# Two transformer layers on one core: input split straight from PSUM, key copies on ScalarE, shift products and low parts moved, last sum on TensorE

## The chip, the cores and the metric

The kernel runs on one core of a Trainium2 chip, in one launch. The time is what the device takes from start to end, in microseconds, as the median of several runs. The engines of the core are TensorE (PE in the profile, its weight loads PEld), VectorE (DVE), ScalarE (ACT), GpSimd (POOL) and SyncE (SP, which here only issues transfers). Each runs its own list of instructions in order, and they wait for one another through semaphores.

## What is computed

1024 tokens (32 sequences of 32) of width 128 pass through two layers. Cut to what matters:

```
x = x + moe16(moe8(x, cond))             # layer 0: 8 experts (2 of them taken) + a shared one, then 16 (4 taken) + a shared one
a = ln(attention(ln(x) * g_norm))        # layer 1: 16 heads of 64 queries, one key/value head, one extra null key
                                         # q, k = l2norm(..)*scale; sim = 8 q k + rel_pos_bias + null bias, causal
w, idx = top_k(a @ router_W + b, 2);  gates = softmax(w)
h = ((a - mean) * rstd)[:, :, None] * ln_g + ln_b            # one norm per expert (8 experts)
y = gelu(h @ W1 + b1) @ W2 + b2 + a
out = x + sum_e gates_e * y_e
```

## The kernel before

Every large product is made exact to fp32 with three matrix products of the reduced type fp32r: a number x is split into a high part (a cast) and a low part (x minus the cast), and `three` (L903 to L905) adds high*high, low*high and high*low. So each operand costs a cast, mostly on ScalarE, and a subtraction, on VectorE or GpSimd. Tokens are held as two halves of 512 or eight tiles of 128. There is no scheduler: each engine's list is written out by hand, and the order of the statements in a block is the order in which the engine takes them.

The stages, in the order of time:

1. Layer 0's experts (to about 72 us): a loop over blocks of up-projections (`up_unit`, six products of 128x512 each, two PSUM buffers), ScalarE evaluating the gate half (L703) and VectorE multiplying (`f_unit`, L1457). VectorE also does the routing of the 16 experts between these units, one small linked step after another. After four of the units stands a `shift_bias(e)` (L1024): four small fp32 products W1ᵀ·ln_b of layer 1's expert e, written to PSUM bank 6. `first_bias(0)` (L1513) on VectorE adds b1 to them.
2. The down-projection of layer 0 (L1069), and the norm of layer 1. `turn_tiles` (L1055) turns normed tokens to PSUM; `turned` on VectorE multiplies them by g_norm into `act_T` (L1316), `copy_hi` on ScalarE casts (L641), `query_low` on VectorE subtracts (L1584).
3. The query loop (90 to 124 us) over tiles t. TensorE: `q_rows(t+2)`, `q_turn(t)` (L1123). ScalarE: `q_root` (L736), `q_squares` (L731), `q_turned` (L740). VectorE: `q_sum` (L1595), `q_norm` (L1603). Keys and values come from `kv_rows(s)` (L1102), are copied out of PSUM by VectorE (`key_rows`, L1578) and ScalarE (`value_rows`, L757), and the keys, normed on GpSimd, go back through `turn_keys` and `turned_keys` (L749, L752) into `k_diag`, which all scores need.
4. The attention loop (124 to 173 us): `scores`, `values` (L1209), `project` (L1221); VectorE sums, transposes and norms (L1673 to L1679); GpSimd does `subtract`, `probs` (L590) and `both_rstd` (L608 to L611). Into this loop GpSimd's list also has `split_w2(0)` at t=1, `split_w2(1)` at t=2 (L596) and `low_w1(7)` at t=3 (L537, L539): low parts of weights of layer 1's experts.
5. Layer 1's experts (to 266 us): 16 steps `m_up(k)`, `m_down(k)` of twelve products each, ScalarE's gelu, VectorE's `split_gelu` (L1753, L1757), `weighed` (L1772, product times gate, into `y_tmp`) and `gathered` (L1783, into `y_acc`). The gates are made on VectorE (`route_half(s)`, which ends with a count on `v_z`, then `gates_half(s)`), turned on TensorE (`turn_half_gates`), and spread over all partitions by way of DRAM.
6. The end: transposes of `y_acc` (L1296), the sum with x (L1806), and two output transfers (L447).

What SyncE issues is one list too, and its order matters here. Where it is cut to the second half of the program it reads:

```python
for e in range(M_EXP):                    # W2 of layer 1, L416 to L421
    sp.wait_ge(pool_w1, e + 1)
    sp.wait_ge(act_w1, e + 1)
    sp.wait_ge(pe_b1, e + 1)
    sp.dma_start(w2_stage[:, e], ...)
store_gates(0)                            # L426: waits for v_combT 1, writes 16 KB, waits for it
sp.wait_ge(pe_wo, TILES)
for e in range(6):
    spread_gates(e, 0)                    # L431: 256 KB each, read by weighed
store_gates(1)
```

`pool_w1` counts the `low_w1(e)` that GpSimd has finished. TensorE's list in step 2 of layer 1's experts is `m_up(3)`, `turn_half_gates(1)` (waits for `gates_half(1)`), `m_down(2)` (waits for `weighed(0)` and for `split_gelu(2)`), and VectorE's is `route_half(1)`, `weighed(0)`, `gates_half(1)`, `split_gelu(2, 0)`.

## Time and profile before

| | |
|---|---|
| three runs | 272.82, 275.73 (median), 276.0 us |
| the profiled execution | 273.56 us, of which the span in the trace is 271.8 us |
| busy: PE, DVE, ACT, POOL | 250.7 (92%), 215.9 (79%), 146.3 (54%), 105.3 us (39%) |
| chain that ended last | PE 72%, DVE 13%, POOL 8%, ACT 3% |
| DMA | 14.51 MB, mean 53 GB/s |

TensorE is busy nine tenths of the time, so most of what other engines do lies beside it. Its idle time is in few places: the query loop, the attention loop and the last 6 us. The granted clock is full except in two short stretches. Times in the rows below are microseconds from the span's start; a duration can overlap the next row's start, since instructions are pipelined.

### The profile page before, as it was taken

To read this page: it belongs to the slowest core of one execution; us is meant where nothing else is said; L and a number is where in the kernel's file an instruction comes from. 1 tells how busy PE (TensorE), PEld (TensorE's weight loads), DVE (VectorE), ACT (ScalarE), POOL (GpSimd) and SP (SyncE) were. 2 spreads that over 40 slices of the span, in tenths; PEclk is the share of its full clock that TensorE was granted. 3 is DMA by queue.
4 is the path that set the end of the run, shared out by engine and by line. 5 is a ranking of instruction groups with operands and counts; after the bars stand their busy time and mean duration, and the time that the engine had idled before them with its cause. 6 is when DMAs were issued, how large, how long until landed. Compare 5 with 4: busy or idle time off the path is not lost.

```text
span 271.8 us, 5203 instructions
## 1 busy us (share of the span) xinstructions
PE 250.7 (92%) x1876; PEld 201.0 (74%) x1876; DVE 215.9 (79%) x436; ACT 146.3 (54%) x244; POOL 105.3 (39%) x146
## 2 busy tenths in 40 slices
PE   7898999999999969678999979999999999999992
PEld 6776467867899848567767656878888888888881
DVE  7797868687877498977688677789998888788884
ACT  1675332246630435696444336298687867877550
POOL 2898410133592657632457783622031101101000
PEclk9999999999999997999999979999999999999997
DMA  6993610010300050000300010005192000000002
GB/s 170 240 264 46 220 50 0 5 39 0 52 0 2 0 159 0 0 2 2 113 9 2 2 42 0 2 0 177 64 288 97 2 0 1 0 0 2 1 0 78
DMA packets 25018, 14.51 MB, mean 53 GB/s; under 512 B 11809, under 2 KB 21702, under 8 KB 24993
## 3 DMA queue, kind: packets, MB, share of 16 engines
q1 hardware_dynamic: 24448, 13.89, 18.8%
q0 software_dynamic: 544, 0.29, 0.8%
q8 instruction: 15, 0.25, 0.4%
q14 instruction: 11, 0.08, 0.1%
HBM read 13.55 MB, written 0.62 MB: 52 GB/s over the span
## 4 chain that ended last, share of the span: by engine, by line
PE 72%; DVE 13%; POOL 8%; ACT 3%; issue 2%; POOLq 0%; DVEq 0%
PE ps L903 16%; PE ps L905 16%; PE ps L904 15%; PE ps L1069 5%; PE ps L1000 3%; PE ps L1024 3%; DVE arena L1603 2%; PE ps L964 2%; PE ps L1221 2%; PE ps L1209 2%; PE ps L1151 2%; POOL w_lo L506 2%; POOL rstd L611 2%; POOL arena L590 1%; PE ps L912 1%
## 5 line engine op out<-in xcount | busy, mean ns | idle before, releaser
L843 ACT ACTIVATE att_bias<-ps,bias 128x512 f32<-128x512 f32 x64 | 43.5, 689 | 12.6 <-PE ps L905 12.5
L903 PE MATMUL ps<-act_hi,w_hi 128*128 128x512 f32 x120 | 48.6, 405 | 0.9 <-DVE arena L1364 0.7
L905 PE MATMUL ps<-act_hi,w_lo 128*128 128x512 f32 x120 | 47.0, 392 | 0.0
L904 PE MATMUL ps<-act_lo,w_hi 128*128 128x512 f32 x120 | 46.9, 391 | 0.0
L1757 DVE TENSOR_TENSOR g_lo<-att_bias,g_hi 128x1024 fp32r<-128x1024 f32 x32 | 40.9, 1289 | 0.6
L903 PEld LDWEIGHTS ps<-act_hi,w_hi 128*128 128x128 f32 x120 | 22.5, 188 | 6.4 <-issue 1.8
L905 PEld LDWEIGHTS ps<-act_hi,w_lo 128*128 128x128 f32 x120 | 22.5, 188 | 5.1
L904 PEld LDWEIGHTS ps<-act_lo,w_hi 128*128 128x128 f32 x120 | 22.6, 188 | 4.3
L703 ACT ACTIVATE xc<-ps 128x512 f32<-128x512 f32 x18 | 10.7, 597 | 17.2 <-PE ps L905 17.2
L1414 DVE TENSOR_TENSOR arena<-arena,ps 128x512 f32<-128x512 f32 x24 | 16.1, 683 | 3.4 <-PE ps L964 3.3
L1069 PEld LDWEIGHTS ps<-f_down,arena 128*128 128x128 f32 x144 | 17.8, 192 | 0.6
L1753 DVE CAST g_hi<-att_bias 128x1024 fp32r<-128x1024 f32 x16 | 11.3, 708 | 8.6 <-ACT att_bias L843 8.5
L1069 PE MATMUL ps<-f_down,arena 128*128 128x128 f32 x144 | 18.1, 275 | 0.0
L596 POOL TENSOR_TENSOR w_lo<-w_stage,w_hi 128x512 fp32r<-128x512 f32 x4 | 5.2, 1311 | 31.4 <-ACT w_hi L800 31.4
L850 ACT ACTIVATE g_hi<-att_bias 128x1024 fp32r<-128x1024 f32 x16 | 17.0, 1063 | 0.5
L1221 PE MATMUL ps<-w_out,arena 128*128 128x128 f32 x128 | 17.1, 291 | 0.0
L1457 DVE TENSOR_TENSOR arena<-xc,ps 128x512 f32<-128x512 f32 x18 | 12.4, 687 | 5.7 <-PE ps L905 5.3
L1221 PEld LDWEIGHTS ps<-w_out,arena 128*128 128x128 f32 x128 | 16.4, 207 | 0.3
L506 POOL TENSOR_TENSOR w_lo<-w_stage,w_hi 128x256 fp32r<-128x256 f32 (+1 forms) x16 | 12.6, 819 | 10.3 <-ACT w_hi L647 5.7
L537 POOL TENSOR_TENSOR r_big<-w_stage,vec 128x512 f32<-128x512 f32 x8 | 8.3, 1042 | 17.8 <-ACT w_hi L697 10.7
L596 POOL TENSOR_TENSOR w2b_lo<-w_stage,w2b_hi 128x512 fp32r<-128x512 f32 x4 | 5.6, 1410 | 23.5 <-ACT w2b_hi L800 23.5
L1209 PE MATMUL ps<-arena,v_tok 32*64 32x256 f32 x128 | 10.7, 404 | 3.7 <-DVE arena L1667 2.3
(285 smaller groups left out, 587.8 us busy)
## 6 DMA issues: line engine op xcount, KB each, us to landing
arena<-gate_m SPq DMA_DIRECT2D x16, 256.0 KB, 5.9
w_stage<-in_L_ffn_W SPq DMA_DIRECT2D x9, 256.0 KB, 3.1
w_stage<-in_L_ffn_W SPq DMA_DIRECT2D x1, 1792.0 KB, 8.0
x_tok<-in_x SPq DMA_DIRECT2D x2, 256.0 KB, 3.1
w_stage<-in_L_ffn_w_gate SPq DMA_DIRECT2D x1, 512.0 KB, 4.9
w_stage<-in_L_ffn_w_up SPq DMA_DIRECT2D x1, 512.0 KB, 6.7
w_stage<-in_L_cond_Wq SPq DMA_DIRECT2D x1, 512.0 KB, 6.5
f_down<-in_L_ffn_w_down SPq DMA_DIRECT2D x1, 512.0 KB, 5.9
```

Of the source, the lines that this page charges most:

```text
L506: pool.tensor_tensor(c(w_lo), c(w_stage), c(w_hi).bitcast(f32), ALU.subtract).then_inc(pool_lo, 1)
L843: act.activation(gelu[:, k % 2, b, :], bank(b), ACT.Gelu, bias=bias1[:, c:c + 1])\
L850: act.activation(g_hi[:, k % 2, 2:4, :], gelu[:, k % 2, 2:4, :], ACT.Copy).then_inc(act_ghi, 1)
L903: pe.matmul(dst, wh, xh, start=first, stop=False)
L904: pe.matmul(dst, wh, xl, start=False, stop=False)
L905: return pe.matmul(dst, wl, xh, start=False, stop=last)
L1069: return pe.matmul(bank(6 + s)[:, t * P:(t + 1) * P], f_hid[:, b, cols], f_down[:, b, :], start=first, stop=last)
L1209: pe.matmul(ps[h * DH:(h + 1) * DH, 4 + s // 2, (s % 2) * HB * LEN:(s % 2 + 1) * HB * LEN], v_tok[rows, t, :], pT_buf[rows, t % 2].rearran ...
L1221: pe.matmul(bank(6)[:, 0:P], att_T[:, t % 2, b, :], w_out[:, b, :], start=(b == 0), stop=False)
L1414: dve.tensor_tensor(hid[:, q, cols], hid[:, q, cols], bank(4 + i % 2), ALU.mult).then_inc(v_mul, 1)
L1457: dve.tensor_tensor(f_hid[:, b, s * HW:(s + 1) * HW], g_sb[:, n % 2], bank(2 * (n % 2) + 1), ALU.mult)\
L1757: dve.tensor_tensor(g_lo[:, k % 2, b, :], gelu[:, k % 2, b, :], g_hi[:, k % 2, b, :].bitcast(f32), ALU.subtract).then_inc(v_glo, 1)
```

## The change

- The four `shift_bias(0..3)` leave the expert loop of layer 0 and stand in TensorE's list in the query loop; `first_bias(0)` moves there too, on VectorE. They now wait until ScalarE has copied the first half's keys and values out of bank 6, and `turn_keys` waits for `first_bias(0)`.
- The input of queries: ScalarE casts straight from PSUM with the scale (`input_high`), VectorE makes the low part from PSUM in one instruction (`query_low`), and ScalarE writes the full-precision `act_T` afterwards (`input_scaled`), which `kv_rows` waits for.
- Both key copies go from VectorE to ScalarE; `kv_rows(1)` moves from after `q_turn(1)` to ahead of `q_rows(4)`; `turned_keys(0)` is spread over two turns of the loop, and `turned_keys(1)` and `(2)` stand after it.
- On GpSimd `split_w2(0)` and `(1)` move to t=6 of the attention loop, and `low_w1(7)` behind `low_half(1)`, with a wait for the third count of `v_z`.
- The last step's product is weighed in two halves and added by TensorE with the identity (`last_sum`) instead of by VectorE; the output goes out in three transfers.

```diff
@@ gpsimd
-                if t in (1, 2):
-                    split_w2(t - 1)
-                if t == 3:
-                    low_w1(M_EXP - 1)
                 if t == 6:
                     low_half(0)
+                    split_w2(0)
+                    split_w2(1)
             low_half(1)
+            pool.wait_ge(v_z, 1 + HALVES)
+            low_w1(M_EXP - 1)
@@ scalar
+            def input_high(s):
+                act.wait_ge(pe_xT, 2 + s + 1)
+                act.wait_ge(v_small, 4)
+                cols = slice(s * HW, (s + 1) * HW)
+                act.activation(act_hi[:, cols], bank((4, 7)[s]), ACT.Identity, scale=vec[:, V_GN:V_GN + 1])\
+                    .then_inc(act_hi_s, 1)
+            def input_scaled(s):
+                act.wait_ge(v_lo, 4 + s + 1)
+                cols = slice(s * HW, (s + 1) * HW)
+                act.activation(act_T[:, cols], bank((4, 7)[s]), ACT.Identity, scale=vec[:, V_GN:V_GN + 1])\
+                    .then_inc(act_x, 1)
...
+            def key_rows(s):
+                act.wait_ge(pe_kv, s + 1)
+                act.activation(k_tok[:, s * HT:(s + 1) * HT, :],
+                               bank(6 + s).rearrange("p (t c) -> p t c", c=P)[:, :, 0:DH], ACT.Copy).then_inc(act_k, 1)
...
+            key_rows(0)
+            value_rows(0)
             input_std(1)
             for t in range(TILES):
                 if t == 2:
-                    copy_hi(5)
+                    input_high(1)
+                    input_scaled(1)
...
+                if t == 2:
+                    key_rows(1)
                 if t == 3:
-                    value_rows(0)
                     value_rows(1)
...
-                if 5 <= t:
-                    turned_keys(t - 5)
+                if t in (5, 6):
+                    turned_keys(0, (t - 5,))
+            turned_keys(1)
+            turned_keys(2)
@@ tensor, expert loop of layer 0
-                if 3 <= j < 7:
-                    shift_bias(j - 3)
@@ tensor, query loop
             for t in range(TILES):
                 if t == 1:
                     turn_tiles(1)
+                if t == 2:
+                    shift_bias(1)
+                    kv_rows(1)
                 if t + 2 < TILES:
                     q_rows(t + 2)
+                if t == 1:
+                    shift_bias(0)
                 if t == TILES - 1:
                     scores(0)
                 q_turn(t)
-                if t == 1:
-                    kv_rows(1)
+                if t in (2, 3):
+                    shift_bias(t)
@@ tensor, end
+            for t in range(HT):
+                pe.matmul(last_sum(t), y_acc[:, 1, t * P:(t + 1) * P], ident[:, :], start=(t % 2 == 0), stop=False)
+            for t in range(HT):
+                if t % 2 == 0:
+                    pe.wait_ge(v_y, steps + t // 2)
+                mm = pe.matmul(last_sum(t), y_tmp[:, (steps - 1) % 2, t * P:(t + 1) * P], ident[:, :],
+                               start=False, stop=(t % 2 == 1))
...
@@ vector
             rp_norm(1)
-            first_bias(0)
...
+                dve.scalar_tensor_tensor(act_lo[:, cols], bank((4, 7)[s]), vec[:, V_GN:V_GN + 1],
+                                         act_hi[:, cols].bitcast(f32), ALU.mult, ALU.subtract).then_inc(v_lo, 1)
...
                 if t == 1:
-                    dve.wait_ge(pe_xT, 4)
-                    turned(1, bank(7), 4, scale=vec[:, V_GN:V_GN + 1], lo=False)
-                if t == 2:
-                    key_rows(0)
-                    key_rows(1)
+                    query_low(1)
+                if t == 4:
+                    first_bias(0)
```

How GpSimd's list changes between the attention loop and the end; L596 is `split_w2`, L537 and L539 are `low_w1`, L602 is `low_half`, L590 is `probs`:

```order
 L611 TENSOR_TENSOR rstd<-var,half_neg 128x2 [waits pool_chain]
-L537 TENSOR_TENSOR r_big<-w_stage,vec 128x512 [waits pool_w1,act_w1]
-L539 TENSOR_TENSOR w_lo<-r_big,w_hi 128x512 [waits pool_chain]
 L590 TENSOR_TENSOR arena<-arena,ssum 128x512 [waits v_pT,v_rs]
...
 L602 TENSOR_TENSOR act_lo<-act_T,act_hi 128x512 [waits act_xhi]
+L596 TENSOR_TENSOR w_lo<-w_stage,w_hi 128x512 [waits act_w2]
+L596 TENSOR_TENSOR w2b_lo<-w_stage,w2b_hi 128x512 [waits act_w2]
...
 L602 TENSOR_TENSOR act_lo<-act_T,act_hi 128x512 [waits act_xhi]
+L537 TENSOR_TENSOR r_big<-w_stage,vec 128x512 [waits pool_w1,act_w1,v_z]
+L539 TENSOR_TENSOR w_lo<-r_big,w_hi 128x512 [waits pool_chain]
```

`low_w1(7)` stood ahead of a `probs` in the middle of the attention loop and now stands behind everything of that loop, with a wait for `v_z`.

SyncE's list is not touched there; in the changed program it reads (L422 is the transfer of W2, L427 `store_gates`, L432 `spread_gates`):

```order
L422 DMA w_stage<-in_L_ffn_W 128x4x128 [waits pe_b1,act_w1,pool_w1] x8
L427 DMA gate_m<-comb_T 32x128 [waits v_combT]
L432 DMA arena<-gate_m 128x512 [waits pe_wo,ld_gate_mw]
L432 DMA arena<-gate_m 128x512 x5
L427 DMA gate_m<-comb_T 32x128 [waits v_combT]
```

All eight transfers of W2 stand ahead of the first `store_gates`, as before.

TensorE's list in the query loop from `q_turn(1)` to `q_rows(4)`, before:

```order
L1123 MATMUL ps<-ident,arena 128x128 [waits act_qT,v_qhat]
L1123 MATMUL ps<-ident,arena 128x128 x7
L1102 MATMUL ps<-w_kv,act_T 128x128 [waits v_T,ld_kv]
L1102 MATMUL ps<-w_kv,act_T 128x128 x3
L903 MATMUL ps<-w_hi,act_hi 128x512 [waits pool_lo,v_qhat,v_lo,act_hi_s]
```

and now (L1051 is `shift_bias`, L1149 `q_turn`, L1126 `kv_rows`):

```order
L1051 MATMUL ps<-vec,w_stage 128x96 [waits act_k,act_v,v_small,ld_w1]
L1051 MATMUL ps<-vec,w_stage 128x96 x3
L1149 MATMUL ps<-ident,arena 128x128 [waits act_qT,v_qhat]
L1149 MATMUL ps<-ident,arena 128x128 x7
L1051 MATMUL ps<-vec,w_stage 128x96 [waits act_k,act_v,v_small,ld_w1]
L1051 MATMUL ps<-vec,w_stage 128x96 x3
L1126 MATMUL ps<-w_kv,act_T 128x128 [waits act_x,ld_kv]
L1126 MATMUL ps<-w_kv,act_T 128x128 x3
L929 MATMUL ps<-w_hi,act_hi 128x512 [waits pool_lo,v_qhat,v_lo,act_hi_s]
```

Two shift products stand ahead of `kv_rows(1)`. On ScalarE `key_rows(1)` stands ahead of `q_root(3)`, so that this root waits for `kv_rows(1)` as well.

## Rows read from the trace of the kernel before

**Rows 1.** Windows: window, length, busy us of PE, PEld, DVE, ACT, POOL, granted clock, DMA share, GB/s

```profile
101.20:105.40 4.20, 3.80 (x13) 3.14 (x14) 4.17 (x6) 1.71 (x3) 4.20 (x4) 0.59 0.02 5
158.20:164.00 5.80, 5.43 (x39) 4.32 (x39) 4.85 (x14) 2.77 (x6) 3.78 (x7) 0.71 0.12 35
200.00:266.00 66.00, 66.00 (x290) 53.81 (x288) 55.96 (x70) 46.30 (x62) 6.97 (x5) 1.00 0.08 29
```

**Rows 2.** Timeline of PE in layer 0's expert loop: start, duration, line, [idle before]

```profile
50.32 1.03 PE L1024 MATMUL ps<-vec,w_stage 128*128 128x96 f32 x8
51.13 0.47 PE L903 MATMUL ps<-act_hi,w_hi 128*128 128x512 f32 x1
```

**Rows 3.** Timeline of DVE in the same loop

```profile
48.30 0.69 DVE L1457 TENSOR_TENSOR arena<-xc,ps 128x512 f32<-128x512 f32 x1 [0.77 <-PE ps L905]
52.86 0.69 DVE L1457 TENSOR_TENSOR arena<-xc,ps 128x512 f32<-128x512 f32 x1 [1.11 <-PE ps L905]
```

**Rows 4.** Timeline of PE at the first queries and in the query loop

```profile
89.99 0.47 PE L903 MATMUL ps<-w_hi,act_hi 128*128 128x512 f32 x1 [0.34 <-issue]
...
100.10 0.66 PE L1055 MATMUL ps<-ident,arena 128*128 128x128 f32 x4 [1.67 <-DVE arena L1566]
101.60 0.77 PE L903 MATMUL ps<-w_hi,act_hi 128*128 128x512 f32 x1 [0.85 <-DVE arena L1603]
...
104.30 1.38 PE L1123 MATMUL ps<-ident,arena 128*128 128x128 f32 x8
105.52 1.06 PE L1102 MATMUL ps<-w_kv,act_T 128*128 128x128 f32 x8
```

**Rows 5.** Timeline of ACT in the query loop

```profile
108.20 0.22 ACT L736 ACTIVATE rn<-n 128x16 f32<-128x16 f32 x1 [1.45 <-DVE n L1595]
```

**Rows 6.** Timeline of POOL in the attention loop

```profile
148.31 1.27 POOL L596 TENSOR_TENSOR w2b_lo<-w_stage,w2b_hi 128x512 fp32r<-128x512 f32 x1
...
154.21 1.04 POOL L537 TENSOR_TENSOR r_big<-w_stage,vec 128x512 f32<-128x512 f32 x1
155.33 1.27 POOL L539 TENSOR_TENSOR w_lo<-r_big,w_hi 128x512 fp32r<-128x512 f32 x1
```

**Rows 7.** The page's costliest groups: line L1209 (`values`), busy and mean | idle before, releaser

```profile
L1209 PE MATMUL ps<-arena,v_tok 32*64 32x256 f32 x128 | 10.7, 404 | 3.7 <-DVE arena L1667 2.3
```

**Rows 8.** Timeline of DVE: one line alone and beside GpSimd's work

```profile
36.29 0.28 DVE L1421 TENSOR_TENSOR rp_early<-rp_early 63x128 f32<-63x128 f32 x1
...
56.59 1.28 DVE L1421 TENSOR_TENSOR rp_early<-rp_early 63x128 f32<-63x128 f32 x1
```

**Rows 9.** Timeline of SP's issues: start of the first, stretch to the last's end

```profile
95.50 61.49 SPq L421 DMA_DIRECT2D w_stage<-in_L_ffn_W  x8
183.51 0.34 SPq L426 DMA_DIRECT2D gate_m<-comb_T  x1
184.93 2.72 SPq L431 DMA_DIRECT2D arena<-gate_m  x6
```

**Rows 10.** The view of line L421 (W2 transfers): issue to landing

```profile
DMA to landing us min/median/max: 2.6/3.6/4.9
```

**Rows 11.** The view of line L426 (the gates' store): issue to landing

```profile
DMA to landing us min/median/max: 1.4/1.4/1.4
```

**Rows 12.** The view of line L431 (the gates' spreading): issue to landing

```profile
DMA to landing us min/median/max: 3.1/5.9/6.7
```

**Rows 13.** Timeline of DVE at the first steps of layer 1's experts

```profile
189.98 0.74 DVE L1772 SCALAR_TENSOR_TENSOR k_diag<-ps,vec,arena 128x512 f32<-128x512 f32 x1
...
192.09 2.36 DVE L1757 TENSOR_TENSOR g_lo<-att_bias,g_hi 128x1024 fp32r<-128x1024 f32 x2
```

**Rows 14.** Timeline of PE there: the start of `m_down(2)`

```profile
193.71 0.48 PE L903 MATMUL ps<-g_hi,w_hi 128*128 128x512 f32 x1
```

**Rows 15.** Timeline of DVE at the end

```profile
265.80 0.75 DVE L1772 SCALAR_TENSOR_TENSOR k_diag<-ps,vec,arena 128x512 f32<-128x512 f32 x1 [0.94 <-PE ps L905]
268.02 0.69 DVE L1806 TENSOR_TENSOR x_tok<-x_tok,ps 128x512 f32<-128x512 f32 x1 [0.15 <-PE ps L1296]
```

More of the change, by code:

```diff
@@ L444, in _ @@
                 spread_gates(e, 1)
[L445 to L446 removed]
+            for n, (t, w) in enumerate(((0, HT), (HT, HT // 2), (HT + HT // 2, HT // 2))):
+                sp.wait_ge(v_out, n + 1)
                 sp.dma_start(out.rearrange("b s c -> (b s) c").rearrange("(t p) c -> p t c", p=P)
[L448 to L450 removed]
+                             [:, t:t + w, :], x_tok[:, t:t + w, :]).then_inc(ld["out"], 16)
+            sp.wait_ge(ld["out"], 48)
         @block.gpsimd
@@ L1121, in q_turn @@
                     pe.wait_ge(act_qT, t)
+                else:
+                    pe.wait_ge(act_x, 1)
                 for b in range(HB):
@@ L1308, in link, with turned @@
                 dve.wait_ge(v_chain, n_chain[0])
-            def turned(s, src, base, scale=None, lo=True):
+            def turned(s, src, base, lo=True):
                 cols = slice(s * HW, (s + 1) * HW)
-                if scale is None:
-                    dve.tensor_copy(act_T[:, cols], src).then_inc(v_T, 1)
-                else:
-                    dve.tensor_scalar(act_T[:, cols], src, scale, None, ALU.mult).then_inc(v_T, 1)
+                dve.tensor_copy(act_T[:, cols], src).then_inc(v_T, 1)
                 if lo:
@@ L1787, in residual, with weighed_last @@
                                          ALU.mult, ALU.add).then_inc(v_res, 1)
-            for k in range(steps):
+            def weighed_last():
+                e, s = m_steps[steps - 1]
+                dve.wait_ge(pe_m_down, steps)
+                dve.wait_ge(m_gate_in[e][s], 16)
+                for n in range(2):
+                    c = slice(n * HW // 2, (n + 1) * HW // 2)
+                    dve.scalar_tensor_tensor(y_tmp[:, (steps - 1) % 2, c], bank(4 + (steps - 1) % 2)[:, c],
+                                             vec[:, V_B2 + e:V_B2 + e + 1],
+                                             m_gate[:, e, s * HW + c.start:s * HW + c.stop], ALU.add, ALU.mult)\
+                        .then_inc(v_y, 1)
+            for k in range(steps - 1):
                 weighed(k)
```

63 lines of the change are left out of this document (27 added, 36 removed).

## The prediction

> **What bounds the kernel now.** I read the page's busy row first (TensorE 92%), then windows by stage, the chain of waits, and the timelines of each engine where TensorE is not full. From 200 to 266 us TensorE is busy 66.00 of 66 us at a granted clock of 1.00 [rows 1]: what is lost before that stretch is lost for good, and what is gained there is gained. The other stages are mixed. In layer 0's expert loop VectorE's linked routing steps and TensorE take turns as the limit; in the query loop VectorE's chain; in the attention loop a ring of VectorE's norm, GpSimd's rstd and `probs`, and VectorE's transpose, with TensorE close behind. Twice TensorE's mean granted clock is 0.59 and 0.71 of full [rows 1], that is, part of those stretches at 1.2 GHz and part at 2.4.
>
> All clock times below are of the profiled execution before (273.56 us in all). I move stage by stage and add.
>
> **Shift products out of the expert loop.** One of the four takes TensorE 0.81 us, 50.32 to 51.13 [rows 2], so 4 x 0.81 = 3.2 us at most. But VectorE waits for TensorE only 0.77 and 1.11 us in that stretch [rows 3]; everything else is its own work, and a block's two PSUM buffers tie TensorE to it. Once those waits are gone VectorE is the limit. `first_bias(0)` leaves too, about 0.1. Gain: 0.77 + 1.11 + 0.1 = **-2.0** (bounds -3.2 and 0). TensorE idles there in pieces of about 1.2 us instead.
>
> **The input of queries.** A chain of three (scale, cast, subtract) becomes two, some 0.9 us shorter. But TensorE is in the down-projection until 0.34 us before the first query product at 89.99 [rows 4], so only 0.34 counts. It is inside the next term.
>
> **The query loop.** VectorE loses a scaling and two key copies, about 2 us of a chain that set the pace. TensorE gets four shift products, 3.2 us, at the very place where its clock is low: after waits of 1.67 and 0.85 us it comes back at half speed, six products of `q_rows(3)` taking 101.60 to 104.30 = 2.70 us and the turn another 1.22 [rows 4]. Nothing in the change touches those two waits, so I expect the low clock again. Then, starting at 101.26: `q_rows(3)` to 103.96, `shift_bias(0)` partly at the low clock 1.3 to 105.3, `q_turn(1)` 0.9 to 106.2, `shift_bias(1)` 0.8 to 107.0, `kv_rows(1)` about 1.0 [rows 4] to 108.0. ScalarE's `key_rows(1)` can only follow, to 108.4, and `q_root(3)` stands behind it in ScalarE's list. It began at 108.20 before [rows 5], so VectorE's gain is gone and 0.25 with it. Two more shift products (1.6 us) then stand ahead of `q_rows(5)` and `q_rows(6)`, and `first_bias(0)` makes VectorE wait for the fourth ahead of `q_sum(5)`: I put another 0.85 on that. ScalarE's copies of keys are only reordered; the same copies stand ahead of the first scores. Sum **+1.1**. Bounds: -2.3 if VectorE's saving passes whole, +2.9 if all four products lie on the path less the 0.34. If the clock stays full the same walk gives -0.8.
>
> **The attention loop.** GpSimd's two `split_w2` of 1.27 us and `low_w1(7)`, 154.21 to 156.60 = 2.4 [rows 6], leave the ring: 4.9 us. Not all of it is gained, since TensorE is nearly full there. Its products `values` waited 2.3 us in sum for VectorE's transposes [rows 7], most of it once, behind `low_w1(7)`; I take 2.2 as gained. Right after that wait came the second low-clock stretch: 5.80 us at 0.71 [rows 1] is (1 - 0.71) x 5.80 = 1.7 us of lost clock. 2.2 + 1.7 = 3.9 gained. Against it, the two splits now stand ahead of `both_rstd(6)` and beside VectorE's `route_half(0)`. What such company costs shows in one line of VectorE that takes 0.28 us alone and 1.28 beside GpSimd [rows 8]; I take 0.9. Sum **-3.0** (bounds -3.9 and -2.3). The Trainium skill (SBUF — State Buffer, Who interferes with whom) says that a VectorE instruction with two SBUF inputs and a GpSimd instruction that reads SBUF exclude each other; by it the first step of `route_half(0)` would wait for the whole second split, 1.27, and the sum would be 0.4 higher.
>
> **What `low_w1(7)` holds up where it now stands.** It waits for the third count of `v_z`, the end of `route_half(1)`, which is where `weighed(0)` began, at about 190.0 [rows 13]. It takes 2.4 us [rows 6]: 192.5 with the hand-over. SyncE's list is unchanged, and its eighth W2 transfer waits for `pool_w1` 8, that is, for `low_w1(7)`. Before, that wait ended at 156.6 (95.50 plus 61.49 [rows 9] is the end of the last of the eight), 27 us ahead of `store_gates(0)` at 183.51 [rows 9]. Now `store_gates(0)` is behind it. So: W2's issue at 192.5; 0.4 later the store, which lands 1.4 after its issue on an empty queue [rows 11] and, right behind 256 KB whose own landing takes 2.6 at least [rows 10], hardly before 195.4 (194.3 by the first row, 196.1 to 197.4 by W2's median and maximum). Then the first spreading, 3.1 us at best [rows 12]: 198.5. Only then can `weighed(0)` run, which ran at 189.98 [rows 13]. From it to the first half of `split_gelu(2)` are 192.09 + 1.2 - 189.98 = 3.3 us [rows 13], so `m_down(2)` starts at 201.8 where it started at 193.71 [rows 14]; TensorE has nothing else in its list. Cost **+8.0**. At least +7.0 (store as before), at most about +11.5 (store 1, first spreading at the median of 5.9 [rows 12], 2.8 above the minimum). All else keeps its distance: `gates_out(1)` and the second store move by the same amount, and after 200 us VectorE has 10 us of room in 66 [rows 1].
>
> The Trainium skill (DMA: Bandwidth & Descriptors, Queues, rings and completion order) says that the transfers of one issuing engine share a ring on each DMA engine and that descriptors there are consumed in order. By it the store waits for W2's packets, as taken; without it the stall would be 1.0 us shorter, 278.1 in all.
>
> **The clock after that stall.** TensorE idles 8 us. The row for the low stretch after the shorter waits of the query loop gives (1 - 0.59) x 4.20 = 1.7 us lost [rows 1]. Cost **+1.7** (0 to +2).
>
> **The last sum.** Before: weighing at 265.80, a sum, four transposes, and the last sum with x at 268.02 to 268.71 [rows 15]. Now, after 265.60, TensorE does four transposes and eight small fp32 products, about 0.45 + 8 x 0.22 = 2.2 us by the 1.06 us of eight passes of L1102 [rows 4], then a half-size sum of 0.4: about 268.4. **-0.3**. Between 0 and -0.9, with the smaller last transfer.
>
> **Sum.** -2.0 + 1.1 - 3.0 + 8.0 + 1.7 - 0.3 = +5.5, so 273.56 + 5.5 = **279.1 us**. The profiled execution lies 2.2 below the median 275.73 and 0.7 above the fastest run, 272.82; on the mean of the four, 274.5, the sum gives 280.0. I say 279.3. Against the median that is 1.3%, against the profiled run 2.0%. About 2% (5.5 us) is what a measurement of this kernel can tell from no change.
>
> **The cases.**
>
> A. As summed, a stall of some 8 us with gains of 4 to 5 beside it: 276 to 281. Chance 0.50, the forecast. For it: SyncE's list and the rows of its waits. Against: the gains rest on hand walks.
>
> B. Ends on the other side, slower by over 2%: the same stall, with the spreading as the long piece. The six spreadings of 256 KB share the DMA engines with W2's 256 KB; if the first lands at the median of 5.9 us and the store with W2's median, `m_down(2)` starts at 193.7 + 11.5. The sum is then +9.0, 282.6. It decides from a stall of about 9 us on (279.1 + 1.3 over the line of 281.2 needs +2.1). For it: the store is now behind a large transfer, and the baseline may be nearer 274. Against: before, the first spreading evidently landed near its minimum, since `weighed(0)` did not wait. Chance 0.33.
>
> C. The query loop keeps its clock because it restarts with denser work: -1.9 against A, 277.2. The two waits ahead speak against it. Chance 0.10 (the side is A's).
>
> D. The stall is not there, since VectorE's `weighed(0)` finds its gates in time: only if W2's eighth transfer is not waited for in the order of SyncE's list. Then 279.1 - 8.0 - 1.7 = 269.4, or 267.5 with C, faster by 1.5 to 2.2% against the profiled run. Chance 0.07; the 61.49 us over which the eight issues are strewn [rows 9] show that the queue does stand still for each.
>
> Chances: faster by over 2% 0.06; within 2% 0.53 (A less its upper edge, C, part of D); slower 0.41 (B and A's upper edge). Range 275 to 283.5: C less a microsecond of the runs' scatter, up to B plus one.
>
> **What would show it.** SyncE's eighth W2 issue near 188 us (192.5 less the 4 gained before) with `store_gates(0)` right behind it; one wait of VectorE of 7 to 9 us ahead of the first L1772-like instruction, and of TensorE at the start of `m_down(2)`, with a clock near 0.6 for some 4 us after. In the expert loop, waits of VectorE for TensorE near zero and the down-projection some 2 us earlier. In the query loop, ScalarE's root of tile 3 held by the key copy; `probs` directly behind `both_rstd` in the attention loop, and no low clock there. I am wrong if `weighed(0)` does not wait, or if the stretch up to the first scores is shorter by more than 3 us.

## The result

The changed kernel takes **280.36 us** (median of four runs, 280.26 to 281.15) against 275.15 for the kernel before (four runs, 272.82 to 276.0). The ratio is 1.021, 95% interval 1.014 to 1.028: it is slower, and whether by more or less than 2% the interval leaves open. Ratios here and below leave out executions more than 1.5% above the fastest of the same kernel. Forecast were 279.3 us and a range of 275.0 to 283.5. The profiled execution took 280.45 us, with a span of 278.7 against 271.8.

Where the two traces part can be read from a few fixed points of the program (us from the span's start). "The stage alone" is a row's difference less that of the row above it, and "forecast" is the prediction's term for it:

| point | before | after | difference | the stage alone | forecast |
|---|---|---|---|---|---|
| start of VectorE's `f_unit(8)`, the ninth of the expert loop of layer 0 | 57.89 | 55.60 | -2.3 | -2.3 | -2.0 |
| first `values` (end of the query loop) | 131.20 | 130.33 | -0.9 | +1.4 | +1.1 |
| end of `route_half(1)` (end of the attention loop) | 190.06 | 185.59 | -4.5 | -3.6 | -3.0 |
| start of `m_down(2)` | 193.71 | 198.12 | +4.4 | +8.9 | +8.0 |
| TensorE past the last product of layer 1's experts (start of what follows) | 265.60 | 272.44 | +6.8 | +2.4 | +1.7 |
| end of the span | 271.8 | 278.7 | +6.9 | +0.1 | -0.3 |

Of the first -2.3, 0.14 stood there before the loop began. The change gains 4.5 us up to the end of the routing and loses 11.3 directly behind it.

### The profile page after: what moved, and what is told of

Read it like the earlier page. It is cut to its first block, busy times and chain, and to the rows that moved or that the text cites. A ratio compares the mean times of both kernels' runs of the same rounds, so it can differ in the third digit from the quotient of the medians.

```text
span 278.7 us, 5238 instructions
## 1 busy us (share of the span) xinstructions
PE 251.7 (90%) x1888; PEld 201.9 (72%) x1888; DVE 212.5 (76%) x433; ACT 148.0 (53%) x248; POOL 103.5 (37%) x146
## 4 chain that ended last, share of the span: by engine, by line
PE 65%; DVE 14%; POOL 9%; DMA 4%; ACT 3%; issue 3%; SPq 1%; DVEq 0%; POOLq 0%; ACTq 0%
PE ps L929 12%; PE ps L931 12%; PE ps L930 12%; PE ps L1094 5%; PE ps L1178 3%; PE ps L1253 3%; PE ps L1026 3%; PE ps L1241 3%; POOL w_lo L506 3%; PE ps L1051 3%; PE ps L990 2%; PE ps L1149 2%; DMA w_stage<-in_L_cond_w_up 1%; DVE g_lo L1784 1%; DMA arena<-gate_m 1%
## 5 line engine op out<-in xcount | busy, mean ns | idle before, releaser
L1784 DVE TENSOR_TENSOR g_lo<-att_bias,g_hi 128x1024 fp32r<-128x1024 f32 x32 | 38.9, 1225 | 1.2 <-ACT g_hi L876 0.6
L1780 DVE CAST g_hi<-att_bias 128x1024 fp32r<-128x1024 f32 x16 | 12.0, 750 | 10.9 <-ACT att_bias L869 10.9
L596 POOL TENSOR_TENSOR w_lo<-w_stage,w_hi 128x512 fp32r<-128x512 f32 x4 | 5.2, 1297 | 35.6 <-ACT w_hi L826 35.6
L1799 DVE SCALAR_TENSOR_TENSOR k_diag<-ps,vec,arena 128x512 f32<-128x512 f32 x15 | 11.2, 745 | 9.4 <-DMA arena<-gate_m 9.4
L537 POOL TENSOR_TENSOR r_big<-w_stage,vec 128x512 f32<-128x512 f32 x8 | 8.3, 1040 | 22.6 <-ACT w_hi L697 10.7
L929 PE MATMUL ps<-g_hi,w_hi 128*128 128x512 f32 x32 | 13.8, 432 | 2.0 <-DVE g_lo L1784 1.9
L1253 PE MATMUL ps<-w_out,arena 128*128 128x128 f32 x128 | 15.6, 275 | 0.0
L1498 DVE TENSOR_TENSOR arena<-xc,ps 128x512 f32<-128x512 f32 x18 | 12.3, 686 | 3.8 <-PE ps L931 3.5
L1253 PEld LDWEIGHTS ps<-w_out,arena 128*128 128x128 f32 x128 | 15.0, 192 | 0.1
```

The costliest lines, as they stand in the source:

```text
L929: pe.matmul(dst, wh, xh, start=first, stop=False)
L1253: pe.matmul(bank(6)[:, 0:P], att_T[:, t % 2, b, :], w_out[:, b, :], start=(b == 0), stop=False)
L1498: dve.tensor_tensor(f_hid[:, b, s * HW:(s + 1) * HW], g_sb[:, n % 2], bank(2 * (n % 2) + 1), ALU.mult)\
L1780: dve.tensor_copy(g_hi[:, k % 2, b, :], gelu[:, k % 2, b, :]).then_inc(v_ghi, 1)
L1784: dve.tensor_tensor(g_lo[:, k % 2, b, :], gelu[:, k % 2, b, :], g_hi[:, k % 2, b, :].bitcast(f32), ALU.subtract).then_inc(v_glo, 1)
```

## The profile after

The windows view of the changed kernel (columns as in [rows 1]) shows the stretches that answer to [rows 1], and those in which the clock now falls:

```profile
98.00:102.00 4.00, 3.27 (x23) 3.04 (x24) 3.63 (x5) 2.43 (x5) 4.00 (x4) 1.00 0.00 0
120.50:125.50 5.00, 4.46 (x128) 3.99 (x132) 1.41 (x2) 2.77 (x5) 1.08 (x1) 0.66 0.01 3
182.00:205.00 23.00, 14.68 (x53) 11.32 (x52) 12.80 (x25) 8.96 (x14) 2.97 (x3) 0.78 0.37 121
198.00:203.00 5.00, 4.88 (x12) 3.85 (x13) 4.97 (x7) 0.00 (x0) 0.00 (x0) 0.50 0.17 55
204.00:272.00 68.00, 68.00 (x298) 55.46 (x297) 55.73 (x69) 48.85 (x66) 7.80 (x6) 1.00 0.09 31
```

From 182 to 205 us TensorE is busy 14.68 of 23 us, and from 198 to 203 it runs at 0.50, the lower level of 1.2 GHz. From 204 on it is full again, 68.00 of 68: nothing that was lost can be made up, as [rows 1] said of the kernel before.

Who stands still at that place is read from SyncE's timeline, which answers to [rows 9]:

```profile
101.31 87.17 SPq L422 DMA_DIRECT2D w_stage<-in_L_ffn_W  x8
188.53 0.49 SPq L427 DMA_DIRECT2D gate_m<-comb_T  x1
191.13 2.72 SPq L432 DMA_DIRECT2D arena<-gate_m  x6
```

The eight W2 transfers now reach to 188.5 (101.31 + 87.17), where they ended at 157.0 before. `store_gates(0)` is issued right behind the eighth, 5.0 us later than before, and the first spreading 2.6 us after that. GpSimd's timeline shows what the eighth waited for:

```profile
185.66 1.04 POOL L537 TENSOR_TENSOR r_big<-w_stage,vec 128x512 f32<-128x512 f32 x1 [5.63 <-DVE r_z L1730]
186.78 1.30 POOL L539 TENSOR_TENSOR w_lo<-r_big,w_hi 128x512 fp32r<-128x512 f32 x1
```

`low_w1(7)` waits 5.63 us for the end of `route_half(1)` (VectorE's L1730, 185.39 + 0.20), and starts at once then. VectorE's timeline, to be held against [rows 13]:

```profile
194.64 0.75 DVE L1799 SCALAR_TENSOR_TENSOR k_diag<-ps,vec,arena 128x512 f32<-128x512 f32 x1 [9.05 <-DMA arena<-gate_m]
...
196.75 2.36 DVE L1784 TENSOR_TENSOR g_lo<-att_bias,g_hi 128x1024 fp32r<-128x1024 f32 x2
```

`weighed(0)` waits 9.05 us for the spread gates, where it had waited for nothing. TensorE's timeline, against [rows 14]:

```profile
195.86 0.37 PE L1281 MATMUL ps<-ident,comb 128*32 128x128 f32 x1 [6.43 <-DVE comb L1738]
198.12 0.77 PE L929 MATMUL ps<-g_hi,w_hi 128*128 128x512 f32 x1 [1.89 <-DVE g_lo L1784]
```

A row of the page: it names a DMA as the releaser behind a VectorE line, 9.4 us in sum, which no row of the page did before:

```profile
L1799 DVE SCALAR_TENSOR_TENSOR k_diag<-ps,vec,arena 128x512 f32<-128x512 f32 x15 | 11.2, 745 | 9.4 <-DMA arena<-gate_m 9.4
```

Landings of the store (L427) in the changed kernel, against [rows 11]:

```profile
DMA to landing us min/median/max: 1.4/2.0/2.6
```

The 2.6 is the first store, right behind W2's 256 KB (whose own landings are 2.6 to 3.1); the 1.4 is the second, on an empty queue.

The other stages. TensorE's timeline in the expert loop, against [rows 2]:

```profile
50.90 0.47 PE L929 MATMUL ps<-act_hi,w_hi 128*128 128x512 f32 x1 [0.99 <-DVE arena L1498]
```

Now TensorE waits for VectorE, and VectorE for nobody (against [rows 3]; L1498 is the line of [rows 3]'s L1457):

```profile
50.07 1.29 DVE L1498 TENSOR_TENSOR arena<-xc,ps 128x512 f32<-128x512 f32 x2
52.83 0.68 DVE L1498 TENSOR_TENSOR arena<-xc,ps 128x512 f32<-128x512 f32 x1
```

TensorE's timeline in the query loop, against [rows 4]:

```profile
97.23 0.66 PE L1080 MATMUL ps<-ident,arena 128*128 128x128 f32 x4 [1.68 <-DVE arena L1606]
98.73 0.47 PE L929 MATMUL ps<-w_hi,act_hi 128*128 128x512 f32 x1 [0.85 <-ACT act_hi L728]
...
117.18 1.06 PE L1149 MATMUL ps<-ident,arena 128*128 128x128 f32 x8 [0.81 <-ACT arena L754]
...
121.04 1.63 PE L1178 MATMUL ps<-k_diag,arena 128*32 128x66 f32 x64 [2.68 <-ACT k_diag L766]
122.59 1.97 PE L1149 MATMUL ps<-ident,arena 128*128 128x128 f32 x8
```

The same two waits as before, 1.68 and 0.85, but the next product takes 0.47 and not 0.77: the clock stayed full. It falls 22 us later, behind a wait of 2.68 for the keys (1.56 before), and the query's turn takes 1.97 instead of 1.09. ScalarE's timeline, against [rows 5], shows the hold-up forecast for `q_root(3)`, the root that stands directly behind the key copy; VectorE waits 1.00 us for it:

```profile
103.92 0.39 ACT L772 ACTIVATE arena<-ps 128x256 f32<-128x256 f32 x1 [0.76 <-PE ps L1126]
104.20 0.21 ACT L750 ACTIVATE rn<-n 128x16 f32<-128x16 f32 x1
```

And in the attention loop GpSimd's two splits (against [rows 6]) stand ahead of `both_rstd(6)`:

```profile
167.20 1.28 POOL L596 TENSOR_TENSOR w_lo<-w_stage,w_hi 128x512 fp32r<-128x512 f32 x1
168.43 1.28 POOL L596 TENSOR_TENSOR w2b_lo<-w_stage,w2b_hi 128x512 fp32r<-128x512 f32 x1
```

Beside the second of them runs VectorE's first step of `route_half(0)`:

```profile
168.60 1.17 DVE L1720 TENSOR_TENSOR r_z<-logits,rstd 128x32 f32<-128x32 f32 x1
...
182.90 0.18 DVE L1720 TENSOR_TENSOR r_z<-ps,rstd 128x32 f32<-128x32 f32 x1
```

It ends with the split (169.77 against 169.71) and is 1.0 us longer than the same step in `route_half(1)`, when GpSimd is idle.

## The experiments

All ratios are to the kernel before in runs on the same chip, with 95% intervals.

**Only W2's last transfer moved.** Theory: the loss is one stall, made by the order of SyncE's list. The changed kernel with the eighth W2 transfer behind all spreadings; this is called the repaired kernel below.

```diff
-            for e in range(M_EXP):
+            for e in range(M_EXP - 1):
                 load_w2(e)
...
                 spread_gates(e, 1)
+            load_w2(M_EXP - 1)
```

> The changed kernel, with one line moved in SyncE's list: the eighth transfer of W2 (the one that waits for low_w1(7)) is issued behind all spreadings of gates. Theory 1 (the store of the gates is held by that transfer): VectorE's wait of 9.05 us ahead of weighed(0) goes, m_down(2) follows m_up(3) without a gap, the clock stays full there; 280.4 - 9.0 (stall) - 2.4 (low clock) = 269.0 us, ratio to the kernel before 0.978. Rival (the gates are late for another reason, such as the late second half of the routing, or the spreadings are slow in themselves): the wait stays above 5 us, the time above 275.

Measured: 270.05 us (269.93 to 271.81), ratio 0.985 (0.978 to 0.992). SyncE's timeline of this kernel (L430 the store, L435 the spreading, line numbers four higher):

```profile
179.12 0.34 SPq L430 DMA_DIRECT2D gate_m<-comb_T  x1
180.55 2.72 SPq L435 DMA_DIRECT2D arena<-gate_m  x6
...
197.80 1.17 SPq L422 DMA_DIRECT2D w_stage<-in_L_ffn_W  x1
```

The store goes out 9.4 us earlier than in the changed kernel, while `low_w1(7)` is where the change put it. VectorE's timeline has `weighed(0)` with no wait at all:

```profile
185.51 0.74 DVE L1803 SCALAR_TENSOR_TENSOR k_diag<-ps,vec,arena 128x512 f32<-128x512 f32 x1
```

Moving one transfer in SyncE's list gives back 10.3 us between the medians (10.5 between the two traces) and turns a kernel 2% slower into one 1.5% faster. The stall and the low clock behind it account for all of the loss.

The kernel is 1.0 us above the 269.0 expected, and its trace shows where. `low_w1(7)` now runs beside the steps of `gates_half(1)`, two of which grow from 0.18 and 0.16 us (the same steps in the changed kernel, at 195.30 and 195.82) to 0.58 and 1.05. VectorE's timeline, then GpSimd's:

```profile
186.17 0.58 DVE L1741 SCALAR_TENSOR_TENSOR r_z<-r_s,r_rank 128x32 f32<-128x32 f32 x1
...
187.10 1.05 DVE L1745 TENSOR_TENSOR g_sum<-g_sum,rstd 128x4 f32<-128x4 f32 x1
```

```profile
185.67 1.04 POOL L541 TENSOR_TENSOR r_big<-w_stage,vec 128x512 f32<-128x512 f32 x1 [5.61 <-DVE r_z L1734]
186.79 1.33 POOL L543 TENSOR_TENSOR w_lo<-r_big,w_hi 128x512 fp32r<-128x512 f32 x1
```

From the end of `route_half(1)` to `m_down(2)` it takes 4.7 us here, against 3.65 in the kernel before. So the new place of `low_w1(7)` has a price of its own, 1.0 us, which the stall had covered in the changed kernel; the prediction has no term for it.

**`low_w1(7)` back in the attention loop.** The changed kernel, SyncE's list as in it:

```diff
+                if t == 3:
+                    low_w1(M_EXP - 1)
...
             low_half(1)
-            pool.wait_ge(v_z, 1 + HALVES)
-            low_w1(M_EXP - 1)
```

> The changed kernel with low_w1(7) back at t=3 of the attention loop, all else as changed, SyncE's list untouched. Theory 1: the stall goes here too, but GpSimd's 2.4 us stand in the loop again: TensorE waits about 1.6 us there and perhaps runs at the low clock for some us; 269.0 + 1.6 + 1.5 = 272 us. Rival (the stall comes from the splits or the later order of GpSimd, not from the wait on v_z): the wait of VectorE ahead of weighed(0) stays.

Measured: 272.08 us (269.82 to 273.16), ratio 0.989 (0.982 to 0.997). The store goes out at 182.35, and the stall is gone this way too; the attention loop has its wait again, 0.64 us where the kernel before had 1.57. TensorE's timeline:

```profile
157.04 0.66 PE L1241 MATMUL ps<-arena,v_tok 32*64 32x256 f32 x8 [0.64 <-DVE arena L1694]
```

So either end of the coupling can be cut. Cutting it on SyncE's side reads 2 us better in the medians, but the intervals of the two overlap, and in this profiled execution the clock was low at the queries as well (first product 0.77 at 99.05). The two traces differ by 2.25 us at the end of layer 1's experts: 0.3 are there before the queries, 1.4 arise in the query loop, whose program is the same in both, 1.5 are `low_w1(7)` in the attention loop, and 1.0 comes back because nothing runs beside the gates. What the choice of the end itself is worth is thus about 0.5 us in these traces, less than can be told.

**Only `low_w1(7)` moved, in the kernel before.** If the stall is this one move, it should make the whole loss by itself.

```diff
-                if t == 3:
-                    low_w1(M_EXP - 1)
...
             low_half(1)
+            pool.wait_ge(v_z, 1 + HALVES)
+            low_w1(M_EXP - 1)
```

> The kernel before with nothing changed but low_w1(7), moved behind low_half(1) with its wait for the third count of v_z. Theory 1: + 9.0 for the stall, + 2.0 for the low clock after it, - 1.6 for TensorE's wait in the attention loop and - 1.7 for the low clock behind that: 275.2 + 7.7 = 283 us, ratio 1.028. Rival (the stall needs the other parts of the change): within 2 us of the kernel before.

Measured: 280.64 us (280.24 to 283.66), ratio 1.024 (1.016 to 1.032), 2.4 below the time expected. SyncE's timeline, then VectorE's:

```profile
188.73 0.37 SPq L421 DMA_DIRECT2D w_stage<-in_L_ffn_W  x1
189.15 0.49 SPq L426 DMA_DIRECT2D gate_m<-comb_T  x1
191.73 2.72 SPq L431 DMA_DIRECT2D arena<-gate_m  x6
```

```profile
194.99 0.75 DVE L1772 SCALAR_TENSOR_TENSOR k_diag<-ps,vec,arena 128x512 f32<-128x512 f32 x1 [8.79 <-DMA arena<-gate_m]
```

One move makes the same stall as the whole change and the same time. The trace is 7.0 us longer than that of the kernel before (278.8 against 271.8), where the terms expected gave 7.7; most of the 2.4 us that the expectation was off lies in its starting point, the median of 275.2, where the profiled execution took 273.56. The wait of `weighed(0)` begins at 186.20 (194.99 - 8.79). From the first `values`, at 130.47, that is 55.7 us, against 58.9 before and 55.3 in the full change: taking `low_w1(7)` out of the attention loop brings 3.1 of the 3.6 us that the loop gains.

**Only GpSimd's moves, with W2's last transfer behind.** The kernel before, with the three moves of GpSimd's list and SyncE's list as repaired; queries' input, keys, shift products and last sum as before.

```diff
@@ gpsimd
-                if t in (1, 2):
-                    split_w2(t - 1)
-                if t == 3:
-                    low_w1(M_EXP - 1)
                 if t == 6:
                     low_half(0)
+                    split_w2(0)
+                    split_w2(1)
             low_half(1)
+            pool.wait_ge(v_z, 1 + HALVES)
+            low_w1(M_EXP - 1)
@@ sync
+            load_w2(M_EXP - 1)      # behind the spreadings
```

> The kernel before with all three moves on GpSimd (both split_w2 and low_w1(7)), and W2's eighth transfer behind the spreadings. Measures the attention term by itself: predicted -3.0, read as -3.7 from the two traces: 275.2 - 3.7 = 271.5 us, ratio 0.987. If the gain is only that of TensorE's single wait behind low_w1(7), -1.6; if all 4.9 us of GpSimd's work were on the path, -4.9.

Measured: 270.66 us (270.60 to 270.88), ratio 0.985 (0.980 to 0.991), the same ratio as the repaired kernel. What the shift products, queries' input, keys and last sum bring beside GpSimd's moves can't be told from zero in these runs: 0.6 us in the medians, with intervals some 2 us to either side, and -2.3 + 1.4 + 0.1 = -0.8 in the table. The trace has the attention loop 3.6 us shorter than before and the way from `route_half(1)` to `m_down(2)` 1.0 longer, as in the repaired kernel.

**Shift products back in the expert loop.** The repaired kernel, with `shift_bias(0..3)` and `first_bias(0)` where they were.

```diff
+                if 3 <= j < 7:
+                    shift_bias(j - 3)
...
             for t in range(TILES):
                 if t == 2:
-                    shift_bias(1)
                     kv_rows(1)
-                if t == 1:
-                    shift_bias(0)
-                if t in (2, 3):
-                    shift_bias(t)
```

> The kernel with W2's eighth transfer behind the spreadings (270.05 us, called the repaired kernel from here on), with the four shift products and first_bias(0) back in the expert loop of layer 0, all else as repaired. Theory 1 (the products give 2.1 us in the expert loop and cost nearly as much in the query loop, where VectorE waits 1.00 us for the root of tile 3 and 0.67 us for the fourth product): + 2.1 - 1.7 = + 0.4, that is 270.5 us, and both waits are gone from the trace. Rival (the query loop hides them, so the whole 2.1 us is lost): 272.2 us.

Measured: 271.44 us (269.29 to 275.06, ten runs), ratio 0.991 (0.987 to 0.995), between the two expectations. VectorE's two waits, 1.00 us for the root and 0.67 for the fourth product, are gone from the trace, as expected. The ratios lie 0.6% apart, and the intervals of this kernel and of the repaired one overlap (0.987 to 0.995 against 0.978 to 0.992): that the move of the shift products gains or costs anything in the whole kernel is not shown.

**The first scores behind the last query turn.** The 2.68 us wait has a simple reading: ScalarE's last copies of keys now stand behind the loop and finish at 120.9, and `q_turn(7)`, whose input was ready, stands behind `scores(0)` in TensorE's list. So in the repaired kernel the two are exchanged.

```diff
-                if t == TILES - 1:
-                    scores(0)
                 q_turn(t)
+                if t == TILES - 1:
+                    scores(0)
```

> The repaired kernel with scores(0) behind q_turn(7) in TensorE's list instead of ahead of it. TensorE waits 2.68 us for the last copy of keys with q_turn(7) queued behind, and runs at the low clock after. Theory 1: the turn (1.0 us at full clock, 1.9 at the low one) falls into the wait, which shrinks to 1.7 us, and less work is left at the low clock: - 1.0 to - 2.4, 267.7 to 269.0 us. Rival (ScalarE sets the pace, since its last q_turned follows a table load of 1.28 us in either order): within 0.5 us of 270.0.

Measured: 269.58 us (267.87 to 269.96), ratio 0.984 (0.979 to 0.990). TensorE's timeline:

```profile
120.99 1.09 PE L1153 MATMUL ps<-ident,arena 128*128 128x128 f32 x8 [1.15 <-DVE arena L1638]
122.52 2.05 PE L1182 MATMUL ps<-k_diag,arena 128*32 128x66 f32 x128 [0.44 <-ACT k_diag L770]
```

The wait is 1.15 and 0.44 in place of 2.68, and the clock stays full there. In this execution it fell at the queries instead (first product at 98.78 us, 0.76 long), so the profiled kernel starts this stretch 1.5 us late and still has its scores done at about 124.6, where the changed kernel needs until 125.8. In the medians the gain is 0.5 us, less than can be told; it is what the rival gave, and not the 1.0 to 2.4 of the expectation.

**The last sum back on VectorE.** The repaired kernel with the end of the program as before: two transfers, all sixteen steps weighed and gathered on VectorE.

```diff
-            for k in range(steps - 1):
+            for k in range(steps):
                 weighed(k)
...
-            weighed_last()
+            dve.tensor_tensor(xs, xs, bank(6 + s), ALU.add).then_inc(v_out, 1)
```

> The repaired kernel with the last sum on VectorE again and two output transfers. Theory 1 (from the two traces: the sum itself ends 0.27 us sooner with TensorE's, and the third transfer gives 0.33 back): no difference in time, 270.0 us; from the last product of layer 1's experts to the end of the span 6.2 us against 6.26. Rival (as predicted, 0.3 us gained by the change): 6.5 us and 270.4.

Measured: 271.81 us (269.85 to 273.16, ten runs), ratio 0.990 (0.986 to 0.994). From the end of the last product to VectorE's last addition it takes 3.11 us (263.93 to 267.04) and in the repaired kernel 2.85 (262.17 to 265.02), but from the same start to the end of the span 6.17 and 6.03. VectorE's end in this kernel, then in the repaired one:

```profile
264.12 0.75 DVE L1792 SCALAR_TENSOR_TENSOR k_diag<-ps,vec,arena 128x512 f32<-128x512 f32 x1 [0.94 <-PE ps L936]
...
266.35 0.69 DVE L1837 TENSOR_TENSOR x_tok<-x_tok,ps 128x512 f32<-128x512 f32 x1 [0.15 <-PE ps L1333]
```

```profile
262.37 0.88 DVE L1826 SCALAR_TENSOR_TENSOR k_diag<-ps,vec,arena 128x256 f32<-128x256 f32 x2 [0.94 <-PE ps L935]
...
264.15 0.87 DVE L1849 TENSOR_TENSOR x_tok<-x_tok,ps 128x256 f32<-128x256 f32 x2 [0.31 <-PE ps L1342]
```

So the last sum gives 0.26 us, and about half of that goes to the third output transfer: SyncE's issues take 1.91 us instead of 1.22. (Between the kernel before and the changed one nothing of it is left, 6.20 and 6.26 us.) The 1.8 us between the medians arise ahead of the end: in the profiled execution the granted clock from 96 to 108 us was 0.86 here and 1.00 in the repaired kernel, and the order of work there is the same in both. They say nothing about the last sum.

**The turned keys copied in the loop, as before.** The repaired kernel, with ScalarE's copies at their old places.

```diff
-                if t in (5, 6):
-                    turned_keys(0, (t - 5,))
-            turned_keys(1)
-            turned_keys(2)
+                if 5 <= t:
+                    turned_keys(t - 5)
```

> The repaired kernel with the copies of turned keys in the loop as before (one whole piece at each of t = 5, 6, 7). Theory 1 (ScalarE's copies ahead of the first scores are the same in sum): the first scores start within 0.3 us of the repaired kernel's 121.03, TensorE's wait of 2.68 us ahead of them is split into pieces of 1.0 to 1.5, and the low clock behind it (1.5 us of time) goes: 268.5 us. Rival (the new order of the copies is what lets VectorE finish early, and helps): first scores 0.5 to 1 us later, 270.5 to 271.

Measured: 269.07 us (268.65 to 270.23), ratio 0.984 (0.979 to 0.990). The 2.68 us wait became 1.56, for VectorE, as before the change, and the clock from 118 to 128 us was 1.00. The first scores, however, start at 122.87 and not within 0.3 us of 121.03, as expected: in this execution the clock fell at the queries (first product 0.77 at 98.81, clock 0.66 from 98 to 108). The spread-out copies, part of the change, are what made the wait of 2.68; that the kernel gains without them is not shown by the medians.

**Both together, and the old kernel with the same order.** One kernel takes the repaired one with both edits. The other is the kernel with only GpSimd's moves and W2's last transfer behind, and the exchange of `scores(0)` and `q_turn(7)`.

```diff
@@ both: tensor
-                if t == TILES - 1:
-                    scores(0)
                 q_turn(t)
+                if t == TILES - 1:
+                    scores(0)
@@ the first alone: scalar
+                if 5 <= t:
+                    turned_keys(t - 5)
```

> The repaired kernel with both of the small edits that did no harm: scores(0) behind q_turn(7), and the turned keys copied inside the loop as before. If the wait ahead of the first scores is one loss and its two removals each give it back, they don't add: each of them alone ran at 269.58 and 269.07 (repaired alone 270.05), so 268.9 (268.3 to 269.6), ratio about 0.981. If they were separate gains they would add to 268.6 or less; that differs by less than can be told. Shown by the trace either way: no low clock from 118 to 128 us.

> The kernel before with GpSimd's three moves, W2's last transfer behind the spreadings, and scores(0) behind q_turn(7); no shift products moved, queries' input, keys and last sum as before. Theory: the rest of the change is worth only what the expert loop gained (2.15 us) less what the query loop lost (1.4), so this kernel is 0.5 to 1 us above the combined one: 269.9 (269.3 to 270.8). Rival: the rest is worth nothing, the same time as the combined kernel. Second rival, by the expert loop's gain alone: 271.0. The order of the scores should give nothing here, since the kernel before shows no wait of 2.7 us ahead of the first scores.

Measured: the combined kernel 269.62 us (267.92 to 269.81), ratio 0.984 (0.979 to 0.990); the other 271.64 (270.98 to 273.71), ratio 0.993 (0.989 to 0.997). The two edits don't add, as expected. The exchange, on the other hand, reads slower in the old query loop, where I had expected nothing: 1.0 us in the medians against the kernel without it, with intervals that just overlap, and 2.0 against the combined kernel on the same chip. TensorE's timeline there, and then without the exchange:

```profile
123.05 1.69 PE L1127 MATMUL ps<-ident,arena 128*128 128x128 f32 x8 [1.61 <-DVE arena L1607]
124.67 3.04 PE L1155 MATMUL ps<-k_diag,arena 128*32 128x66 f32 x128
```

```profile
123.05 1.13 PE L1155 MATMUL ps<-k_diag,arena 128*32 128x66 f32 x64 [1.55 <-DVE arena L1607]
```

In both orders the first of the two pieces starts at 123.05, since keys and the last query tile become ready within 0.2 us of each other. Two things differ. With the exchange TensorE runs at the low clock behind its wait in this execution (3.04 us for the 128 products that take 2.05 above), which costs 1.45 us here; but the combined kernel has the same exchange behind the same wait of 1.61 and keeps its clock, so this can't be laid to the order. And `scores(0)` ends one query turn later, so that TensorE waits 0.63 to 0.79 us ahead of the first `values` in all three kernels with the exchange, and in none without it. At full clock it takes 8.44 us from the start of the two pieces to the first `values` in the combined kernel, and 7.74 without the exchange in the kernel with GpSimd's moves. So the exchange costs 0.7 us where both inputs come together; only in the repaired kernel, where the keys came 1.4 us after the query tile, does it take the turn into the wait.

None of the later kernels is measurably faster than the repaired one, which beats the kernel before by 1.5%.

The same fixed points in all traces that matter here show which stage holds what (us):

| kernel | `f_unit(8)` to first `values` | to the end of `route_half(1)` | to `m_down(2)` | to past the last product |
|---|---|---|---|---|
| before | 73.3 | 58.9 | 3.65 | 71.9 |
| changed | 74.7 | 55.3 | 12.5 | 74.3 |
| repaired | 74.7 | 55.3 | 4.7 | 71.9 |
| `low_w1(7)` back | 76.1 | 56.8 | 3.7 | 71.9 |
| only GpSimd's moves | 72.8 | 55.3 | 4.7 | 71.9 |
| combined | 72.8 | 55.2 | 4.7 | 71.9 |

The last two were profiled at nearly full clock, 0.996 and 0.997, and spend the same time from `f_unit(8)` on; the combined kernel is 2.5 us ahead at that point (55.54 against 58.03), 0.3 of it since before the expert loop, and stays so to the end (spans of 266.3 and 268.8). In its executions with the clock at 0.997 and 0.998 it took 268.1 and 267.9 us, where the four of the other, at 0.993 to 0.996, took 270.6 to 270.9. This suggests that the rest of the change is worth some 2 us once the long wait ahead of the first scores is gone and the clock stays up. The medians (269.62 and 270.66, on two chips) don't show it, since four of the combined kernel's six executions ran at 0.993 or 0.994.

## Why the prediction was right, and which of its steps were not

- **The stall** (forecast +8.0, measured +8.9) came from the mechanism named and step by step as laid out: `low_w1(7)` at the end of `route_half(1)`, W2's issue 2.5 us later, the store 0.4 behind, the spreading 2.6 behind that, `weighed(0)` 3.5 after the spreading's issue. Taken singly, the small misses are the spreading (3.5 instead of its minimum of 3.1) and the walk from `weighed(0)` to `m_down(2)` (3.48 instead of 3.3). The first experiment removes the stall by the transfer alone, the third makes it by the one move alone. What the step left out is the 1.0 us that `low_w1(7)` costs beside the gates; under the stall it did not count.
- **The store behind W2.** Its landing went from 1.4 to 2.6 us, and back to 1.4 where W2 was behind it; I had taken about 2.5. By the rule of the Trainium skill (DMA: Bandwidth & Descriptors, Queues, rings and completion order), that on each DMA engine the descriptors of one ring are consumed in order, the store's stand behind W2's: the 2.6 agrees with it, though no run here separates this order from a mere sharing of the DMA engines.
- **The low clock after the stall** (forecast +1.7, measured +2.4). I took the price from a stretch that the query loop offered. After the longer wait the clock stayed at 0.50 from 198.1 to 203.4 us, over the twelve products of `m_down(2)`, which took 5.3 us instead of 2.8. The term was 0.7 us too small.
- **The expert loop** (-2.0, measured -2.3 with the 0.14 that was there before) went as said: VectorE's two waits vanished, TensorE idles instead.
- **The query loop** (+1.1, measured +1.4) is where a right number hides a wrong step. The step "nothing in the change touches those two waits, so I expect the low clock again" failed: the waits were the same to 0.01 us and the clock stayed full. By the walk for a full clock the stage would have come out at -0.8. The missing 2.2 us are more than covered by the wait ahead of the first scores, 2.68 us instead of 1.56, and the low clock behind it, (1 - 0.66) x 5.0 = 1.7 us; the other 0.6 is not resolved. I had not seen them because I wrote of ScalarE's key copies that "the same copies stand ahead of the first scores". They do, but the last of them now stand behind the loop. Two misses cancelled, which was luck: two traces with this same query loop, `low_w1(7)` back and the last sum back, had the low clock that I expected, and there the stage came out at +2.8 and +3.0, not +1.1. Case C's condition was met, and its time was not.
- **The attention loop** (-3.0, measured -3.6, and -3.6 again in each later kernel with `low_w1(7)` out of the loop and both splits moved): no wait for `low_w1(7)`, no low clock from 158 to 164 us. The price of the splits beside `route_half(0)`, taken as 0.9, was 1.0 in one instruction. The Trainium skill (SBUF — State Buffer, Who interferes with whom) would have such a VectorE instruction, with two inputs in SBUF, wait for GpSimd's read of SBUF to end: here it ended 0.06 us after the split, so the trace agrees, and so do the two steps beside `low_w1(7)` in the repaired kernel, which end 0.04 and 0.03 us after GpSimd's. What was more than forecast is not settled between the ring and the clock.
- **The last sum** (-0.3, measured +0.1): 0.26 of it is there on VectorE; the third transfer's issue takes at least half of it back.
- **Case B** (slower by over 2%). I let it decide from a stall of about 9 us on, but my own line, 279.1 us plus 2.1, needs one of 10.1. The stall was 8.9, the low clock 0.7 dearer, and the result is at the edge between A and B, as the ratio of 1.021 says.

## What to carry to other kernels

Before moving an instruction, list who counts its semaphore, and what stands behind that waiter in its own list: here a 2.4 us step that nobody needed for tens of microseconds held an unrelated transfer, and by it 16 KB on which the whole core waited. If a step is made late on purpose, move what waits for it behind everything urgent as well. "Late" is no free place either: beside VectorE's gates the same step cost 1.0 us. And when a forecast hits, check it stage by stage: here the total was right with one stage right for the wrong reasons.

## What the runs showed of the hardware

- TensorE waited the same 1.66 to 1.68 us and 0.85 us ahead of `q_rows(3)` in every kernel here. The first product after them took 0.76 or 0.77 us in the kernel before and in five experiments, and 0.47 or 0.48 in the changed kernel and five experiments. With the program up to that point as before the change, it started at 100.93 and 101.60 us low, at 101.67 and 101.72 full; as in the changed kernel, at 98.66 and 98.73 full, at 98.78, 98.81 and 99.05 low, and at 98.91 full for the first product and low soon after (0.86 from 96 to 108 us). So the same program with the same waits meets the low clock in one execution and not in another, and a forecast can only give a chance for it. What decides remains open.
- This is a good part of the scatter between executions of one kernel: of the kernel before, executions with a mean granted clock of 1.000 took 272.3 us, one with 0.982 took 273.5 and one with 0.969 276.2. The kernel with GpSimd's moves alone stayed within 0.3 us in four executions, at 0.993 to 0.996.
- What the low clock cost was not the same everywhere. From the first query product to the first `values` it cost 1.4 to 1.6 us in the changed query loop (44.6 and 44.8 us against 43.2) and 0.5 in the old one (41.2 against 40.7). Why is not shown; VectorE was busy 3.97 of 4 us there from 101 to 105 us, so that TensorE was hardly the engine that set the pace.
- A small VectorE instruction with both inputs in SBUF took 1.17 us beside GpSimd's split and 0.18 alone, another 1.05 beside `low_w1(7)` and 0.16 alone; a 16 KB store right behind a 256 KB load landed after 2.6 us and alone after 1.4.
